# One step less between the stages of a recurrence: when its scan, gates, sums and ranks are issued

## The reference, cut to what matters

```python
y = layernorm(x)
k = y @ Wz + bz;  a = y @ Wh + bh
z = sigmoid(k);   v = z * where(a >= 0, relu(a) + 0.5, sigmoid(a))
h[t] = (1 - z[t]) * h[t-1] + v[t]        # the reference does it in logs
x = x + layernorm(h) * gamma + beta + y
y2 = layernorm(x)                        # the next block's input
logits = y2 @ router_w.T                 # the best 2 of 8 experts per row
```

## Time and profile before

| what | us |
|---|---|
| median of three runs without profiler | 1425.43 |
| profiled execution, from first to last instruction (span) | 1524.2 |
| recurrence's first instruction / first shift / last shift | 973.3 / 979.8 / 1210.0 |
| first instruction of the second experts | 1237.4 |

### The profile page before, as it was taken

How to read it: one execution, slowest core, us unless ns; L and a number is a source line. 1 busy time by engine, 2 the same in 40 slices (tenths; PEclk the granted TensorE clock), 3 DMA queues, 4 the chain that set the end, 5 groups by cost and what they waited for, 6 DMA issues and landing times. The chain is left out here.

```text
span 1524.2 us, 38116 instructions
## 1 busy us (share of the span) xinstructions
PE 1216.6 (80%) x11689; PEld 1017.3 (67%) x11689; DVE 1144.1 (75%) x3833; ACT 967.7 (63%) x2078; POOL 991.9 (65%) x1131
## 2 busy tenths in 40 slices
PE   5889999999999999973788888577787449888850
PEld 3667777777777777753788888455566348788850
DVE  5489999999999999965566665488888546666638
ACT  3588888888888888851555544277777435455420
POOL 4346688888888888777355665237777835666530
PEclk9699999999999999995799997588878669999955
DMA  7211111111111111123222222112222122222228
GB/s 199 86 46 46 48 60 60 60 60 60 59 60 60 60 60 60 39 93 83 73 86 86 81 85 68 49 49 83 73 83 69 45 68 84 86 84 84 77 83 277
DMA packets 99443, 117.19 MB, mean 77 GB/s; under 512 B 17784, under 2 KB 79792, under 8 KB 99248
## 3 DMA queue, kind: packets, MB, share of 16 engines
q1 hardware_dynamic: 70560, 73.57, 16.3%
q0 software_dynamic: 16896, 35.16, 6.8%
q10 hardware_dynamic: 11792, 6.05, 1.4%
HBM read 47.56 MB, written 41.51 MB: 58 GB/s over the span
## 5 line engine op out<-in xcount | busy, mean ns | idle before, releaser
L1153 DVE TENSOR_TENSOR ebuf<-score_banks,region 128x768 f32<-128x768 f32 x256 | 243.6, 951 | 18.8 <-PE score_banks L862 13.1
L1402 ACT ACTIVATE region<-ebuf 128x768 f32<-128x768 f32 x256 | 215.9, 860 | 23.0 <-DVE ebuf L1153 23.0
L1380 ACT CAST copied<-max_banks 128x768 bf16<-128x768 f32 x251 | 201.9, 804 | 15.1 <-PE max_banks L850 12.5
L1842 POOL DMA_INDIRECT choice_rows<-second_yo,second_xg x136 | 133.1, 979 | 112.7 <-PE second_by L1880 69.3
L1842 POOL DMA_INDIRECT choice_rows<-first_yo,first_xg x136 | 130.7, 961 | 114.0 <-PE first_by L1880 65.9
L1694 POOL DMA_INDIRECT expert_rows<-d_rows,a_d_index x112 | 129.4, 1155 | 27.9 <-issue 17.2
L1918 ACT ACTIVATE second_silu<-second_bgu,second_biases 128x256 f32<-128x256 f32 (+1 forms) x144 | 61.0, 466 | 114.3 <-PE second_bgu L1871 66.7
L1918 ACT ACTIVATE first_silu<-first_bgu,first_biases 128x256 f32<-128x256 f32 (+1 forms) x144 | 61.9, 462 | 111.8 <-issue 83.6
L1954 DVE SCALAR_TENSOR_TENSOR second_hT<-second_bgu,second_biases,second_silu 128x256 f32<-128x256 f32 (+1 forms) x144 | 62.1, 464 | 70.3 <-ACT second_silu L1918 37.6
L905 PE MATMUL bankO<-region,vaug 128*32 128x256 f32 (+1 forms) x2048 | 111.1, 334 | 1.9 <-ACT region L1402 1.9
L853 PE MATMUL max_banks<-region_r 32*128 32x256 f32 x502 | 98.3, 388 | 11.9 <-DVE ebuf L1153 7.4
(11 more groups left out here) (369 smaller groups left out, 4531.6 us busy)
## 6 DMA issues: line engine op xcount, KB each, us to landing
region_r<-region_r SPq DMA_DIRECT2D x192, 128.0 KB
first_xg<-expert_rows SPq DMA_DIRECT2D x64, 132.0 KB
second_xg<-expert_rows SPq DMA_DIRECT2D x64, 132.0 KB
z_rows<-choice_rows SPq DMA_DIRECT2D x32, 256.0 KB
c_rows<-choice_rows SPq DMA_DIRECT2D x16, 512.0 KB
out<-xres ACTq DMA_DIRECT2D x16, 256.0 KB
choice_rows<-first_yo,first_xg POOLq DMA_INDIRECT x136
choice_rows<-second_yo,second_xg POOLq DMA_INDIRECT x136
```

The costliest lines, as they stand in the source:

```text
L1153: nc.vector.tensor_tensor(ebuf[:, half_of_ebuf(c, j), :, :], score_banks[:, :, 0:BK], bias32[:, plain(j), :], ALU.add).then_inc(scores_fre ...
L1380: nc.scalar.copy(copied[:, 2 * j:2 * j + 2, :], banks_of_max(c, j)[:, :, 0:BK]).then_inc(maxed_free, 1)
L1402: nc.scalar.activation(p32[:, j % 4, :, :], ebuf[:, half_of_ebuf(c, j), :, :], ACT.Exp).then_inc(exped, 1)
L1842: pool.indirect_dma_start(choice_dram, bass.IndirectOffsetOnAxis(ap=xg[:, i % G, t, E:E + 1].bitcast(I32), axis=0), yo[:, i % 4, t, :], No ...
```

## The change

The pipeline is one step shallower. `values` and `scan` now handle sequence `i-1` in step `i`, so the gates are made and used in the same step; `finish` handles `i-2`, and the routing `i-3`. `scan` stands ahead of `shifts` on VectorE. On TensorE the three sums of `back` are a function of their own, ahead of `rank`; the transposes and products stay behind it. On ScalarE `make_gates` stands ahead of `take_logits`. Choosing falls on odd steps and placing on even ones. There are 38 steps, with `shifts` in 35. The instructions are the same otherwise.

```diff
-        LAST = B + 7
+        LAST = B + 6
         def scans(i):
+            return 1 <= i <= B
+        def ends(i):
             return 2 <= i <= B + 1
-        def ends(i):
+        def sends(i):
             return 3 <= i <= B + 2
-        def sends(i):
-            return 4 <= i <= B + 3
         def norms(i):
-            return i <= B + 3
+            return i <= B + 2
         def chosen_in(i):
+            return (i - 5) // 2 if i % 2 == 1 and 5 <= i <= B + 3 else None
+        def placed_in(i):
             return (i - 6) // 2 if i % 2 == 0 and 6 <= i <= B + 4 else None
...
                     if scans(i):
-                        valued = values(i - 2, q)
+                        valued = values(i - 1, 1 - q)
+                    if scans(i):
+                        scan(i - 1, 1 - q, valued)
                     if norms(i):
                         shifts(i, q)
-                    if scans(i):
-                        scan(i - 2, q, valued)
                     if chosen_in(i) is not None:
                         choose(chosen_in(i))
                     if ends(i):
-                        finish(i - 3, 1 - q)
+                        finish(i - 2, q)
...
-                def back(b, q):
+                def sums(b, q):
                     if b >= 2:
                         pe.wait_ge(done, b - 1)
                     for k, x in enumerate((tiles(b), flat(xl[:, b % 3, :, :]), flat(beta[:]))):
                         nc.tensor.matmul(bh[q][:, 2 * P:4 * P], ident[:], x, start=(k == 0), stop=(k == 2))
+
+                def back(b, q):
                     pe.wait_ge(scanned, b + 1)
...
                     q = i % 2
+                    if scans(i):
+                        sums(i - 1, 1 - q)
                     if placed_in(i) is not None:
                         pe.wait_ge(d_chosen, ranked + 1)
                         pe.wait_ge(d_logits_taken, min(2 * ranked + 3, B))
                         d.rank(ranks).then_inc(d_ranked, 1)
                         ranked += 1
                     if scans(i):
-                        back(i - 2, q)
+                        back(i - 1, 1 - q)
...
-                    if sends(i - 1):
-                        take_logits(i - 5)
                     if gated(i):
                         make_gates(i - 1, 1 - q)
+                    if sends(i - 1):
+                        take_logits(i - 4)
                     if ends(i):
-                        norm_outputs(i - 3, 1 - q, i)
+                        norm_outputs(i - 2, q, i)
```

More of the change, by code:

```diff
@@ L2115, in scans @@
         def scans(i):
+            return 1 <= i <= B
+        def ends(i):
             return 2 <= i <= B + 1
-        def ends(i):
+        def sends(i):
             return 3 <= i <= B + 2
-        def sends(i):
-            return 4 <= i <= B + 3
         def norms(i):
-            return i <= B + 3
+            return i <= B + 2
         def chosen_in(i):
+            return (i - 5) // 2 if i % 2 == 1 and 5 <= i <= B + 3 else None
+        def placed_in(i):
             return (i - 6) // 2 if i % 2 == 0 and 6 <= i <= B + 4 else None
-        def placed_in(i):
-            return (i - 7) // 2 if i % 2 == 1 and 7 <= i <= B + 5 else None
         def second_labels(m):
@@ L2139, in means_free @@
             if sends(i - 2):
-                engine.wait_ge(d_copied, i - 5)
+                engine.wait_ge(d_copied, i - 4)
             elif i >= 2:
@@ L2162, in statistics @@
                     if sends(i):
-                        dve.wait_ge(done, i - 3)
+                        dve.wait_ge(done, i - 2)
                         for t in range(2):
-                            ch.mark(nc.vector.bn_stats(stats[:, q, 4 + t, :], tile(i - 4, t)))
+                            ch.mark(nc.vector.bn_stats(stats[:, q, 4 + t, :], tile(i - 3, t)))
                     if enters(i):
@@ L2170, in statistics @@
                     if ends(i):
-                        dve.wait_ge(h_full, i - 2)
+                        dve.wait_ge(h_full, i - 1)
                         for t in range(2):
-                            ch.mark(nc.vector.bn_stats(stats[:, q, 2 + t, :], bh[1 - q][:, t * P:(t + 1) * P]))
+                            ch.mark(nc.vector.bn_stats(stats[:, q, 2 + t, :], bh[q][:, t * P:(t + 1) * P]))
                     ch.wait(ch.base + ch.n)
@@ L2271, in _ @@
                         nc.gpsimd.tensor_tensor(rs[:, q, :], arg[:, q, :], half[:], ALU.pow).then_inc(rooted, 1)
-                    if i >= 8 and q == 0 and not d.late((i - 8) // 2):
-                        scatter((i - 8) // 2, 1)
+                    if i >= 7 and q == 1 and not d.late((i - 7) // 2):
+                        scatter((i - 7) // 2, 1)
                     if placed_in(i) is not None:
@@ L2344, in _ @@
                     if sends(i):
-                        turn(i - 4)
+                        turn(i - 3)
                     if enters(i):
@@ L2348, in _ @@
                     if sends(i):
-                        router(i - 4, ranked)
+                        router(i - 3, ranked)
                 pe.wait_ge(found, 1)
@@ L2438, in _ @@
                     if sends(i):
-                        apply(i - 4, i)
+                        apply(i - 3, i)
                     if enters(i):
@@ L2442, in _ @@
                     if sends(i):
-                        take(i - 4)
-                        copy(i - 4, i)
+                        take(i - 3)
+                        copy(i - 3, i)
                 act.wait_ge(known, 1)
```

## The result

The kernel after takes 1475.48 us (median of 6 runs, 1467.46 to 1477.05), the kernel before 1424.78 us in the 6 runs beside it. The ratio is 1.0324, with a 95% interval from 1.0295 to 1.0352: slower by 42 to 50 us (the medians differ by 50.7). The forecast was 1471 us.

The account below looks back on a forecast made before the run. No engine was full; a one-step ring through gates, logits, `values` and scan would set the step. 28.6+28x8.5+12.6 = 279.2 us against 230.2 gave +49.0, divided by 1.069 to +45.8: 1471 us, range 1446 to 1507.

Parts of the forecast that it names:

- Ring instead of slack: Whole step: `values` needs gates made in the same step, so shift, norm, gates, `values`, scan, shift set its length.
- Gates ahead of logits, 1.03 us a step: ScalarE: the logits' copy comes fifth behind four gates, done at S+5.14 against S+4.11, costing 1.03 us each step.
- Steps at full clock: Recurrence at full clock: choosing step 7.66 us, placing step 8.01 us, a pair 15.67 us.
- Scan ahead of shifts, 0.73 a step: VectorE: the shift follows the second `values` instruction by 0.45 plus 0.61 us instead of 0.34, costing 0.73 us.
- Sums ahead of ranks: TensorE in placing steps: costs nothing at full clock; at the low clock delays ranks, with the shift at S+10.72.
- The clock: TensorE: about 2.4 us idle makes the clock fall; choosing steps low at 8.9 us, placing full at 8.01, mean 8.5.
- The sum: First to last shift: 28.6+28x8.5+12.6 = 279.2 us against 230.2, so +49.0 us.
- The scaling: Whole kernel: profiled execution exceeds the median by 1.069, so +49.0 us was divided to +45.8, giving 1471 us.
- the clock that holds: Rival for TensorE's clock: sums fill part of the idle time, the clock stays full, 1452 us; chance 0.18.
- The clock that stays low: Rival for TensorE's clock: low in the whole ring, pairs of 19.6 us, 1507 us; chance 0.18.
- the missing ring: Rival for the step: it stays as long as before and one step less saves some 6 us, 1420 us; chance 0.05.
- The faster rival: Rival: VectorE's own work sets 5.90 us steps, logits done by S+4.11, clock kept full, 1398 us; chance 0.04.

Follow-up runs that it names:

- The depth alone: Kernel after with all three orders (shifts before scan, logits before gates, ranks before sums) put back as in the kernel before: 1429.04 us, ratio 1.0022.
- the filling matmuls: Kernel after with five more unread matmuls a step on TensorE, ahead of the scan's transposes: 1448.80 us, ratio 1.0135 to the kernel before.
- the rows with the filling: Three unread matmuls a step added to the kernel before (1425.14 us) and to the shallower pipeline with all three orders as before (1410.72 us).
- all four versions in which it was tried: Unread matmuls added: kernel after 1448.80 us, shallower pipeline with old orders 1410.72, kernel before with scan ahead of shifts 1417.57, kernel before 1425.14.

## Why the prediction was right, and where its steps were off

The direction, the mechanism (a ring of one step, lengthened by the orders, with a clock that falls and rises) and the size were right: 1471 forecast, 1475.48 measured. That the sum comes so near is in part luck, as several terms were off in opposite directions. Point by point:

- **Ring instead of slack: right.** `values` comes behind logits or ranks of its own step in nearly every step, and VectorE idles 2.3 to 2.5 us in the steps shown, more than the 1 to 2 forecast. The depth alone shows the same ring through the gates at 6.4 to 6.5 us, no longer than the step before: the depth closes the ring, but the three orders make it long.
- **Gates ahead of logits, 1.03 us a step: right.** Alone in the kernel before it cost 26.7 us, 0.95 for each of 28 steps. In the kernel after, undoing it gave only 15.6, because `values` then waits for the gates.
- **Steps at full clock: near.** 7.66 and 8.01 were worked out, 7.52 and 7.89 measured with the clock held (0.97).
- **Scan ahead of shifts, 0.73 a step: too dear.** Undone in the kernel after it gave 14.9 us, 0.44 a step, and at the new depth with the other orders as before a step at full clock is 0.43 longer by it. The prediction named the 0.73 that the shift loses and only up to 0.16 of what the early products give back, but the gate matmuls end 0.30 earlier. In the time from first to last shift the order cost only 3.8 us at the new depth and nothing at the old one (-0.9), since the clock fell less often there (0.94 instead of 0.89, 0.86 instead of 0.82).
- **Sums ahead of ranks: right for the kernel after (0.4 us), wrong in the place of its price.** Placing steps whose gate matmuls ran at full clock take 7.89 us with either order; the 0.4 in all is a balance, as the clock is 0.70 instead of 0.75 with ranks first. I let the order bite at the low clock (10.7 us for a placing step). In the profile after, placing steps had their sums at full clock, so that didn't happen; the order costs 0.67 us in a placing step where the logits are early, which the prediction didn't consider, since in its kernel they never were.
- **The clock: right in kind.** It falls behind the idleness of placing steps (2.60 us) and comes back behind the shorter one of choosing steps (0.91). But I priced low choosing steps at 8.9 and placing at 8.01; measured in the pair shown are 8.46 and 8.69: the low gate matmuls end at S+4.27 instead of the S+4.51 taken over from the kernel before, and the low stretch, 10.0 us long, reaches into the placing step. The sum of the pair, 17.15 against 17.0, hid that.
- **The sum:** 279.2 us from first to last shift were worked out, 276.8 measured, in the shortest of the six runs.
- **The scaling was wrong.** I divided the difference by 1.069, taking the long span of the profiled execution for slowness spread by the profiler. It lay in the expert phases of that one execution. Undivided the same sum gives 1425.43+49.0 = 1474.4.

The rivals: the clock that holds (1452 forecast) was built with the filling matmuls and gave 1448.80. The clock that stays low (1507) is ruled out by the mean of 0.75, and the missing ring (1420) by the waits for logits and ranks. The faster rival (5.90 us steps, 1398) fell at the point named for it: the logits are done at 1080.41 in the step shown, S+5.94, not S+4.11. Behind that stands a reason that I had not seen: GpSimd's queue needs about 6.4 us a step, as the rows with the filling show, so 5.90 can occur in one step but not in all. The rule on waits between VectorE operations, by which the scan would have started 0.11 earlier, is borne out by no row: scan started 0.46 behind the second instruction of `values` in the kernel after (1081.86 to 1082.32).

What stays open: why the gains of single orders don't add up exactly. Each order also moves TensorE's idle time, and the clock changes with each; the runs show that, and for scan ahead of shifts what it gives back, but don't separate it for each pair of orders.

## What to carry to other kernels

Taking a step out of a software pipeline turns slack into a ring: before doing it, walk once around from a shared point (here `shifts`) back to it, engine by engine, and compare that length with the step; the step taken out is won once, the ring is paid in every step. Two orders that delay the same consumer hide each other, so an order that is free in one version can cost 0.67 us in every second step of the next. Compare steps of the same clock before you call an order free: 0.43 us a step were nearly hidden by a clock that fell less often. An engine matters by its idle time too, where its clock falls: matmuls that nobody reads were worth 21 us here. And before a forecast is scaled by a long profiled execution, compare it phase by phase with another one.

## What I had not expected of the hardware

Filling TensorE's idle time with useless matmuls held the granted clock at 0.95 to 0.97 of full in all four versions in which it was tried, and made three of them faster: 276.8 to 255.5, 229.8 to 218.7 and 229.3 to 223.2 us from first to last shift. For the third the intervals of the ratios overlap (0.9951 to 1.0000 without, 0.9915 to 0.9974 with), so its gain is shown by the profiles alone. In the fourth, the kernel before, GpSimd's roots took over as the last arrival.
